# Two graph attention layers on one core: the second layer's row gathers wait for the dot products six rows back

## What is computed

```python
h = jnp.maximum(_layernorm(x, axis=-1), 0.0)
x = x + _L0_gnn_ref(h, adj, L0_gnn_W_seq, L0_gnn_a1, L0_gnn_a2, L0_gnn_W_out, L0_gnn_b_out)
h = jnp.maximum(_layernorm(x, axis=-1), 0.0)
x = x + _L1_gnn_ref(h, adj, L1_gnn_W_q, L1_gnn_b_q, L1_gnn_W_k, L1_gnn_b_k, L1_gnn_W_v, L1_gnn_b_v)
```

```python
q = sent_embed @ W_q.T + b_q
k = sent_embed @ W_k.T + b_k
v = sent_embed @ W_v.T + b_v
scale = 1.0 / math.sqrt(sent_embed.shape[-1])
z = scale * (q @ k.T)
spare_z = z * adj_tensor
spare_z = jnp.where(spare_z == 0.0, jnp.asarray(-10000.0, spare_z.dtype), spare_z)
attn = jax.nn.softmax(spare_z, axis=1)
out = attn @ v
return jax.nn.relu(out)
```

## The kernel before

| tile | 4 | 0, 1, 2, 3 | 6 | 8 | 10 | 12 | 14 | 11 | 13 | 15 | 9 | 7 | 5 |
|---|---|---|---|---|---|---|---|---|---|---|---|---|---|
| rows k | none | 0 to 3, one each | 4, 5 | 6, 7 | 8, 9 | 10, 11 | 12, 13 | 14 to 16 | 17 to 19 | 20 to 22 | 23 to 26 | 27 to 31 | 32 to 39 |

## Time and profile before

### The profile page before, as it was taken

The page is one execution under the profiler, slowest core; times in us unless marked ns, Lnnn a source line. Parts: engine busy times, 40 slices in busy tenths (PEclk is TensorE's granted clock), DMA queues, the critical chain, the costliest instruction groups (busy, mean ns, idle before and its releaser), DMA issues.

```text
span 450.1 us, 6244 instructions
## 1 busy us (share of the span) xinstructions
PE 393.3 (87%) x2058; PEld 281.5 (63%) x2070; DVE 368.4 (82%) x731; ACT 245.7 (55%) x511; POOL 255.9 (57%) x268
## 2 busy tenths in 40 slices
PE   7999999998799998999977997978998999968860
PEld 4888887786588886886554755645656855434430
DVE  3999999986899999998799999689854568989900
ACT  4379777783999999872442443343433346142220
POOL 2335151321868866876786535883524777788640
PEclk9599999999899999999996999989999999989995
DMA  8988999710000023435755432763212676679941
GB/s 322 395 347 316 380 313 350 272 50 25 4 6 6 7 29 91 103 112 151 232 155 148 151 95 87 208 208 112 95 47 96 193 207 200 200 171 130 127 61 19
DMA packets 26996, 70.02 MB, mean 156 GB/s; under 512 B 7892, under 2 KB 8148, under 8 KB 24788
## 3 DMA queue, kind: packets, MB, share of 16 engines
q0 software_dynamic: 13056, 38.45, 32.4%
q1 hardware_dynamic: 13904, 31.16, 19.0%
q10 hardware_dynamic: 4, 0.00, 0.0%
HBM read 52.47 MB, written 17.13 MB: 155 GB/s over the span
## 4 chain that ended last, share of the span: by engine, by line
POOL 28%; DVE 16%; issue 15%; PE 11%; DMA 2%; ACT 1%; DVEq 0%; POOLq 0%
PE psum L1349 7%; POOL s_shared L1271 7%; POOL s_shared L1300 5%; POOL out_dram L1284 4%; POOL s_shared L1252 3%; POOL s_rs L1282 3%; DVE s_shared L814 3%; DVE s_shared L812 3%; DVE s_shared L1044 3%; POOL s_x L1290 2%; POOL s_early L1300 2%; PE psum L1450 2%; DVE s_x L828 2%; DVE s_shared L821 1%; DVE h_t L1044 1%
## 5 line engine op out<-in xcount | busy, mean ns | idle before, releaser
L1101 ACT ACTIVATE s_shared<-psum,seq_all 128x320 bf16<-128x320 f32 x192 | 81.9, 571 | 6.0 <-PE psum L1349 4.3
L1349 PE MATMUL psum<-s_shared 128*128 128x198 bf16 x768 | 75.1, 254 | 9.6 <-POOL s_shared L1252 9.6
L1349 PEld LDWEIGHTS psum<-s_shared 128*128 128x128 bf16 x768 | 67.9, 98 | 17.4 <-POOL s_shared L1252 9.9
L563 PE MATMUL psum<-w_seq,hT 128*128 128x272 f32 x256 | 63.3, 402 | 0.4 <-ACT w_seq L424 0.4
L1371 PE MATMUL psum<-w_out,hT 128*128 128x512 f32 x128 | 61.4, 625 | 0.4
L563 PEld LDWEIGHTS psum<-w_seq,hT 128*128 128x128 f32 x256 | 49.0, 195 | 10.2 <-ACT w_seq L424 0.5
L1393 PE MATMUL psum<-w_qk,s_early 128*128 128x257 f32 x240 | 54.5, 379 | 0.0
L1393 PEld LDWEIGHTS psum<-w_qk,s_early 128*128 128x128 f32 x240 | 44.3, 189 | 6.0
L1271 POOL DMA_INDIRECT s_shared<-seq_dram,tab x30 | 37.4, 1246 | 11.3 <-issue 8.9
L1371 PEld LDWEIGHTS psum<-w_out,hT 128*128 128x128 f32 x128 | 26.2, 205 | 26.3 <-issue 25.4
L282 POOL TENSOR_TENSOR rstd<-veps,power 128x1 f32<-128x1 f32 x16 | 8.9, 558 | 54.9 <-DVE veps L468 54.9
(11 more groups left out here) (267 smaller groups left out, 742.1 us busy)
## 6 DMA issues: line engine op xcount, KB each, us to landing
adj_ring<-in_adj_dram SPq DMA_DIRECT2D x16, 1024.0 KB, 7.8
seq_dram<-seq_all POOLq DMA_DIRECT2D x16, 264.0 KB, 4.0
x_ring<-in_x_dram SPq DMA_DIRECT2D x16, 256.0 KB, 8.2
h_dram<-h_t SPq DMA_DIRECT2D x16, 256.0 KB, 2.3
w_seq<-in_L_gnn_W_seq_dram SPq DMA_DIRECT2D x1, 1024.0 KB, 5.5
w_q<-in_L_gnn_W_q_dram SPq DMA_DIRECT2D x1, 1024.0 KB, 13.5
w_k<-in_L_gnn_W_k_dram SPq DMA_DIRECT2D x1, 1024.0 KB, 15.7
w_v<-in_L_gnn_W_v_dram SPq DMA_DIRECT2D x1, 1024.0 KB, 8.6
```

The costliest lines, as they stand in the source:

```text
L563: last = pe.matmul(bank[2 + 2 * (t % 2) + i][:, 0:SX // 2], hT[:, t % 2, c * P:(c + 1) * P], w_seq[:, c, i * (SX // 2):(i + 1) * (SX // 2) ...
L1101: last = act.activation(ind[i][:, j, PAD:], bank[4 + i][:, 0:LN], ACT.Sign, bias=seq_all[:, j, D + n:D + n + 1])
L1349: last = pe.matmul(acc(i)[:, k, 0:3 * W2], ind[i][:, j, k * P:(k + 1) * P], rhs.rearrange("p t w -> p (t w)"), start=(j == 0 and k != 1), ...
```

## The change

Each gather of the second layer from k = 7 on now waits for `dot_done`. The value is k - 6, but at most the number of rows that stand ahead of the gather's own tile: the dots of a tile begin only when all its rows have landed, so a gather can't wait for a dot of its own tile. Nothing else changes, and no instruction moves. For instance k = 13 waits for 7 dots, k = 21 for 15, k = 34 for 28, and k = 38 and 39 for 32.

```diff
         FLAT_ROWS = RING * SG // D
 
+        LEAD = 6
         ROWS_EARLY = FLAT_ROWS + C + LONE + 1
...
                 def gather1(t):
                     for s in range(SLOTS[t]):
                         k = ROW1[t] + s
+                        if min(k - LEAD, ROW1[t]) > 0:
+                            pool.wait_ge(dot_done, min(k - LEAD, ROW1[t]))
                         if k == ROWS_EARLY:
                             pool.wait_ge(u_done, U_NO[EARLY - 1] + 1)
                         if k == ROWS_AGAIN:
```

## The result

The changed kernel takes 464.7 us in the median of four runs (462.28 to 465.4), the kernel before 454.6 (453.88 to 454.87). The ratio is 1.0215, with an interval of 1.0174 to 1.0256: 2.2% slower. The prediction was 464.8 us.

The account below looks back on a forecast made before the run. POOL's gathers were taken to bound the kernel to 398 us, then VectorE. A shift of 9.6 us plus 0.5 for TensorE's clock made 10.1, so 462.1 profiled; plus 2.68 to the median, 464.8 us, range 462.4 to 467.2.

Parts of the forecast that it names:

- Two signs at the end of the prediction: VectorE idle before tiles 15, 9, 7, 5 some 10 us; tile 5's first dot to span end 47.7 to 48.5.
- The bound: POOL's queue of gathers bounds to 398 us, VectorE only 0.84 us behind, then VectorE; delaying gather 39 moves the whole tail.
- Gather 13: Waits for the seventh dot, ending at 367.43; starts at 367.8 instead of 364.11, and nothing depends on it.
- The first stall: Gather 21 waits for tile 11's first dot, ending at 382.71; starts at 383.1, 8.5 us late.
- The second stall: Gather 34 waits for tile 7's first dot; starts at 401.1 instead of 400.0 at pitch, costing 1.1 us.
- The clock: TensorE's low clock after idling, on the product behind tile 13: 1.7 lost, 1.2 won back, 0.5 us net.
- The median: 464.8 us: the predicted profiled execution of 462.1 plus the 2.68 us offset of before, added unchanged.
- Quick gathers (1): Spread-out gathers land in 3.5 us at a pitch of 1.25: shift 8.1 us with the clock, 462.8 us; chance 0.17.
- Dear waits (2): Met waits cost 0.05 us each, wake-ups 0.74, low clock twice as long: 13.1 us, 467.8 us; chance 0.11.
- No change (4): All waits met early, so gathers aren't held; needs the fifteenth dot before 374.6 us; chance 0.02.
- Faster (3): Spread gathers slow VectorE's dots and aggregations of 402.38 to 427.35 less, winning over 10.1 of 24.97 us; chance 0.02.

Follow-up runs that it names:

- the repeat: The changed kernel, unchanged, measured once more beside the kernel before: 464.76 us against 453.32, ratio 1.0253.
- One_pause: Kernel before with one added wait, gather 13 for 7 dots; all other gathers run freely: 456.27 us against 453.32, ratio 1.0072.
- first_only: Changed kernel, but only gathers 7 to 27 wait and 28 to 39 run freely: 463.92 us, before 485.44; run again 464.02, before 484.25.
- Filled: Changed kernel plus 24 unused TensorE products in the idle time before tile 13's transposes: 468.63 us, kernel before 484.47, ratio 0.9679.
- last_first: Kernel before, no added waits, with TensorE taking tile 7's product ahead of tile 5's transposes: 484.59 us, kernel before 484.47, ratio 0.9934.
- lead10: Changed kernel with a lead of 10 rows instead of 6: 464.72 us, kernel before 485.44, ratio 0.9576.
- lead14: Changed kernel with a lead of 14 rows instead of 6: 467.16 us, kernel before 485.44, ratio 0.9618.
- second_only: Changed kernel, but only gathers 34 to 39 wait: 480.4 us, kernel before 485.44; run again 487.18, kernel before 484.25.

## Why the prediction was right, step by step

In order, with the prediction's number and what the first trace has:

| step | predicted | measured |
|---|---|---|
| gather 13 starts | 367.8 | 367.95 |
| last of the gathers 14 to 20 starts | 377.8 | 378.05 |
| gather 21 starts, first real stall | 383.1 | 383.19 |
| dots of tile 15 begin | 388.3 | 389.24 |
| gather 31 starts | 396.1 | 396.28 |
| first dot of tile 7 begins | 400.0 | 401.20 |
| gather 34 starts, second stall | 401.1 | 402.17 |
| gather 39 starts | 407.6 | 408.80 |
| dots of tile 5 begin | 412.0 | 413.14 |
| later by, at tile 5 | 9.6 | 10.76 |
| TensorE's clock, net | 0.5 | 1.48 |
| profiled execution | 462.1 | 464.09 |

Two signs at the end of the prediction: VectorE's idle time before the tiles 15, 9, 7 and 5 is 11.3 us (some 10 was said), and from tile 5's first dot to the end of the span it is 49.2 us in the first trace, outside the stated 47.7 to 48.5, and 47.9 in the repeat, inside.

**The bound was read rightly.** POOL's queue of gathers set the start of tile 5's dots, VectorE being 0.84 us ahead of it, and every later delay of gather 39 came out at the end. One_pause is the direct test: a pause by itself near the beginning, 4.3 us at gather 39, made the kernel 2.95 us slower.

**Gather 13** came as said. The seventh dot was late because VectorE waited for ACT's base of tile 6, 3.10 us in before and 3.41 in after; the prediction named only the aggregation in front of the dot.

**The first stall** is right to 0.1 us. Its start rests on one row of before, the end of tile 11's first dot at 382.71, and on the reason that nothing in front of that dot depends on the gathers; the stretch of VectorE's list ahead of it has no wait for a gather in after either. The dot came 0.2 us later than in before (382.92), and the wake-up, taken as 0.39 us, was 0.27: two small errors that cancel.

**The second stall** was undersized. It was put at 1.1 us. Between gather 31 and tile 7's first dot the prediction took the median landing of 3.9 us; this one took 4.90 by the chain, the longest of its line (3.4/3.8/4.9). That alone is 1.0 of the 1.14 us by which tile 5 came later than predicted. It was no chance: from gather 31 to that dot it is 4.55 to 4.92 us in all eight traces in which VectorE waits for that row. The isolated stall is 1.8 to 2.8 us by first_only. Where two engines wait for each other, each landing counts in full and no slack evens it out, and a value from the middle of the list was too low; VectorE waits for the latest of tile 7's five rows, not for a typical one. The other 0.13 is the pitch of the last five gathers (6.63 against 6.5).

**The clock** was right in its place and its kind, and too small for the first trace. The low clock was expected on the product behind tile 13, and there it is. But TensorE had idled 5.91 us, and the low clock began already at the transposes (1.12 us for 0.66) and lasted through the whole product: 2.8 us lost, where 1.7 had been read from a restart after 3.69 us. The prediction's bounds for it, 0 to 2 net, held it at 1.48. In the repeat the low clock cost 1.45 us on the same two steps and the tail was as long as before's, so there the net term is about 0: the predicted 0.5 lies between the two traces, and which of them comes was not to be read from before. Filled took the term away. A consequence that was not foreseen is VectorE's 1.14 us at 429.24: TensorE was late, so ACT's base of tile 7 was late, and VectorE waited. It cost nothing, as TensorE was behind anyway.

**The median** came out at 464.7, within 0.1 us, by luck: two errors cancel. The trace is 2.0 us above the sum for the profiled execution. The offset of 2.68 us from the profiled execution of before to its median was added unchanged, and proved to be 0.6 in after (464.09 against 464.7): before's profiled execution had been a low one. The right size from median to median is 10.1 us, by the repeat 11.4; the sum was 10.1.

**The rivals.** Quick gathers (1): the least landing fell from 3.5 to 3.4 us and the median from 3.9 to 3.8, but those on the path were 4.9 and 4.3, so it is out. Dear waits (2): the met ones cost nothing (gaps of 0.30), the wake-ups were 0.3 us and not 0.74; only its clock part came half true, and only in the first trace. No change (4) is out, as POOL waited 11.5 us. Faster (3) is out as it was put: dots take 0.69 us with gathers beside them and without, and the stretch from tile 5's first dot to the last output did not get shorter (34.0 and 34.2 us before, 35.4 and 34.1 after). But a faster kernel was possible by another mechanism that the prediction did not have: in the 485-us condition, every kernel of this study whose gathers were made to wait between the gathers 13 and 21 was 3 to 4.5% faster than before, filled with all the waits of the change among them. The trace of before, taken in the 454-us condition, has no sign of it.

## What to carry to other kernels

A wait that keeps a producer in step with its consumer costs the time by which the consumer is late for reasons of its own; look in the consumer's list for the first item that other work holds back, and ask whether the producer's queue bounds the end. Where the two then wait for each other, count each round trip at its long value and not its median. A pause in a queue is swallowed by a later one if that one waits for something which the first doesn't delay, as at the gathers 13 and 21; where it does delay it, both are paid, as at 21 and 34. Put the unchanged kernel beside every comparison, and if its own time has moved, read what that condition does before reading any ratio.

## What the runs showed of the hardware

- A semaphore wait that is met costs nothing on POOL's queue of indirect DMAs: the gap stays 0.30 us. A wait that isn't met ends 0.27 us after VectorE's accumulator read (four times in after). The four gathers that did wait took 1.16 us instead of 0.95; VectorE starts its next dot beside each of them, so the wait itself need not be the reason.
- There is a condition in which the unchanged kernel takes 485 us instead of 454. In last_first's trace, taken in it, TensorE stands still for 19.3 us and VectorE for 22.4, and ACT all but for two copies, while POOL issues gathers without a pause at 207 GB/s; that the unchanged kernel loses its 30 us in the same way is inferred, as it has no trace there. In first_only, lead10 and lead14 ACT went on 1.3 to 2.3 us after POOL paused, but in last_first and second_only it also went on without a pause. The cause is open.
- TensorE's restart after 5.91 us of idle time cost 2.8 us on transposes and one product in one trace and 1.45 after 5.53 us in the repeat, and after 3.69 us it cost 1.7. Twenty-four products that nobody reads, 5.34 us long, took it away, but that kernel had 3.7 us more between its last output and its end.
- POOL's gathers are shorter when VectorE is idle. In before 5 of the 40 gathers have no instruction of VectorE beside them, and take 0.95 to 0.98 us, though TensorE works beside all of them and ACT beside four; the others take 0.95 to 1.34. In last_first the eight gathers into `w_out`, `lone` and `bv_bc` took 0.952 to 0.957 us while VectorE stood still, in before some of the same ones took 1.04, 1.13 and 1.08. The Trainium skill, "SBUF — State Buffer", section on who interferes with whom, says that VectorE's two-input instructions and GpSimd's reads of SBUF contend. The traces agree in the sign, with 0.05 us a gather in the mean of these eight and 0.39 at the most; VectorE's dots show nothing of it, 0.69 us with and without.
